# VectorE's order in a pipelined attention: rests, rotations and sums behind the next step's maximum

## The reference

```python
xn = layernorm(x)
s = mamba2_ssd(xn, ...)                     # layer 0, a chunked selective scan
g = silu(moe_top2(xn, ...))                 # 8 experts, 704 wide
x = x + s * g
xn = layernorm(x)
q = rope(xn @ Wq.T); k = rope(xn @ Wk.T); v = xn @ Wv.T     # 32 query heads, 8 key heads, 64 wide
attn = softmax(causal(q @ k.T / 8)); s = (attn @ v) @ Wo.T  # layer 1
g = silu(sign(layernorm(xn) * gamma + beta) @ sign(W - mean(W)).T * alpha + ...)
x = x + s * g
```

## Time and profile before

| | |
|---|---|
| median of 3 runs | 746.0 us (743.95 to 747.15) |
| the profiled execution | 747.68 us, its span 745.9 us |
| mean granted TensorE clock | 0.986 |
| busy, share of the span | TensorE 92%, VectorE 69%, ScalarE 59%, GpSimd 53% |
| attention and tail | from about 326 us to the end |

### The profile page before, as it was taken

The page is one execution under the profiler, slowest core; times in us unless marked ns, Lnnn a source line. Parts: engine busy times, 40 slices in busy tenths (PEclk is TensorE's granted clock), DMA queues, the critical chain, the costliest instruction groups (busy, mean ns, idle before and its releaser), DMA issues.

```text
span 745.9 us, 13421 instructions
## 1 busy us (share of the span) xinstructions
PE 685.3 (92%) x4447; PEld 600.9 (81%) x4448; DVE 514.4 (69%) x1076; ACT 442.0 (59%) x1075; POOL 392.4 (53%) x442
## 2 busy tenths in 40 slices
PE   2999999999999999699879999999999999999886
PEld 2888999989899897687668878788888888887774
DVE  7583656434423426888868878888788888888755
ACT  4446344243242332457767787877877788777762
POOL 1413542423433332137556787777977778776540
PEclk9999999999999999899999999999999999999999
DMA  8175987786878736154442422333323433242001
GB/s 289 48 245 179 293 261 240 249 266 198 266 248 254 224 104 165 28 163 149 106 124 61 111 72 65 99 83 95 82 65 93 93 78 84 56 103 58 15 16 57
DMA packets 108453, 102.25 MB, mean 137 GB/s; under 512 B 51104, under 2 KB 78688, under 8 KB 108256
## 3 DMA queue, kind: packets, MB, share of 16 engines
q1 hardware_dynamic: 106272, 95.62, 44.8%
q0 software_dynamic: 2112, 5.77, 2.4%
HBM read 69.24 MB, written 11.14 MB: 108 GB/s over the span
## 4 chain that ended last, share of the span: by engine, by line
PE 65%; DVE 20%; ACT 5%; issue 5%; POOL 2%; DMA 1%; SPq 1%; DVEq 0%; ACTq 0%
PE bank L1718 14%; PE bank L1752 8%; PE bank L1570 7%; PE bank L1891 5%; DVE p_lo L1083 3%; PE bank L1858 3%; PE bank L1574 3%; DVE o_rest L1092 3%; PE bank L1575 3%; PE bank L1576 3%; DVE nmax L1074 3%; PE bank L1859 3%; DVE q_mix L1040 2%; PE bank L1903 2%; DVE q_mix L1041 2%
## 5 line engine op out<-in xcount | busy, mean ns | idle before, releaser
L1532 POOL TENSOR_TENSOR prob<-prob,rinv 128x128 f32<-128x128 f32 (+3 forms) x256 | 176.4, 721 | 90.5 <-DVE rinv L1079 90.5
L1334 ACT ACTIVATE prob<-bank,nmax 128x512 f32<-128x512 f32 (+3 forms) x256 | 133.3, 526 | 41.4 <-DVE nmax L1074 29.8
L1083 DVE TENSOR_TENSOR p_lo<-bank,p_hi 128x512 fp32r<-128x512 f32 x160 | 109.3, 683 | 59.1 <-ACT p_hi L1341 57.0
L1341 ACT ACTIVATE p_hi<-bank 128x512 fp32r<-128x512 f32 x160 | 95.4, 596 | 48.6 <-PE bank L1570 47.7
L1718 PE MATMUL bank<-xgT,wm 128*128 128x128 f32 x920 | 111.3, 275 | 0.5 <-ACT xgT L1246 0.5
L1718 PEld LDWEIGHTS bank<-xgT,wm 128*128 128x128 f32 x920 | 108.7, 192 | 3.3 <-issue 1.4
L1858 PE MATMUL bank<-kT,qT 128*128 128x512 f32 (+3 forms) x256 | 83.9, 333 | 19.7 <-ACT prob L1334 15.1
L1570 PE MATMUL bank<-cst,prob 128*128 128x128 f32 x640 | 97.3, 275 | 3.2 <-ACT prob L1334 2.5
L1074 DVE TENSOR_REDUCE nmax<-bank 128x1 f32<-128x512 f32 (+2 forms) x192 | 91.0, 501 | 3.6 <-PE bank L1861 3.6
L1891 PE MATMUL bank<-p_lo,v_parts 128*128 128x256 f32 (+3 forms) x288 | 92.1, 343 | 0.1
L1505 POOL DMA_INDIRECT y_rows<-y_row,to_row x21 | 22.7, 1081 | 108.9 <-DVE y_row L943 86.4
(11 more groups left out here) (319 smaller groups left out, 1530.2 us busy)
## 6 DMA issues: line engine op xcount, KB each, us to landing
wm<-in_w_moe SPq DMA_DIRECT2D x23, 1280.0 KB
wm<-in_w_moe SPq DMA_DIRECT2D x23, 640.0 KB, 5.0
qT<-q_hi SPq DMA_DIRECT2D x124, 64.0 KB, 2.0
qT<-q_lo SPq DMA_DIRECT2D x124, 64.0 KB, 2.0
wo_twice<-wo_hi SPq DMA_DIRECT2D x32, 128.0 KB, 2.5
k_exp<-k_rows SPq DMA_DIRECT2D x56, 64.0 KB, 2.0
wtl<-in_w_moe_tail SPq DMA_DIRECT2D x46, 64.0 KB
y_rows<-gate SPq DMA_DIRECT2D x1, 2048.0 KB, 14.0
```

The source lines that it names most:

```text
L1083: TT(p_lo[:, b_, :], bank[2 + b_ % 2][:, :], p_hi[:, b_, :].bitcast(F32), ALU.subtract).then_inc(plo_done, 1)
L1334: ins = actv(prob[:, i % 2, h, POFF[j]:POFF[j] + (j + 1) * P], bk[:, at:at + (j + 1) * P], ACT.Exp, bias=nmax[:, i % 2, h, j:j + 1], accum ...
L1341: actv(p_hi[:, b_, :], bank[2 + b_ % 2][:, :], ACT.Copy).then_inc(phi_done, 1)
L1532: ins = GT(seg, seg, rinv[:, i % 2, k, j:j + 1].to_broadcast([P, (j + 1) * P]), ALU.mult)
```

## The change

The function that makes the lists gets a switch. With it, seven of VectorE's operations whose place is above 3 are put into the next step, at a place between 2.7 and 2.8: behind that step's maximum S (place 2) and reciprocal N (2.6), and ahead of its T (3). Their order among themselves stays. Only VectorE's calls set the switch, and the tail's list isn't changed by it. Each operation keeps its waits, its signals and its instructions; none is added or removed.

```diff
-def schedule(kind):
+AFTER_MAX = ("R", "W", "r", "qa", "ql", "Vl", "Kr")
+
+def schedule(kind, by_max=False):
...
-    picked = [(n - late * STEPS, p, late, op, i, k) for at, late in lists for n, p, op, i, k in at if (n >= STEPS) == late]
+    def placed(n, p, op, i, k):
+        return (n + 1, 2.7 + p / 100, op, i, k) if by_max and kind != "tail" and op in AFTER_MAX and p > 3 else (n, p, op, i, k)
+
+    picked = [(n - late * STEPS, p, late, op, i, k) for at, late in lists for n, p, op, i, k in (placed(*z) for z in at)
+              if (n >= STEPS) == late]
...
-            attend(0, schedule("first"))
+            attend(0, schedule("first", True))
             for gp in range(KVH // 2 - 1):
                 for a in range(2):
-                    attend(gp * 2 + (1 + a), schedule("middle"))
-            attend(KVH - 1, schedule("last"))
-            attend(KVH, schedule("tail"))
+                    attend(gp * 2 + (1 + a), schedule("middle", True))
+            attend(KVH - 1, schedule("last", True))
+            attend(KVH, schedule("tail", True))
```

## The result

The changed kernel takes 752.52 us (median of 4 runs, 752.34 to 753.06), the kernel before, run beside it, 745.74 us (4 runs, 743.95 to 747.15). The ratio is 1.0079 [1.0051, 1.0107]: slower by 0.8%, more than the bound of 0.5%. The forecast was 747.0 and "no change"; "slower" had a chance of 0.20. 752.52 lies at the range's upper edge (752.5).

A forecast was written before the change was run, and what follows sets the result against it. Attention was taken as nearly TensorE's own work, its idle time tracing to maxima late on a full VectorE. Group 0 +3.0, middle +1.0, group 7 and tail -3.0 gave +1.0: 748.7 profiled, 747.0 against the median; range 742 to 752.5.

The forecast's parts named there:

- The signs that the prediction named: Profile after: S3.3 idle near 0.3, new o_rest waits, Q3.1 waiting about 2 us, W0 near 388.5, a half at 23.8.
- The middle groups: Twelve halves of groups 1 to 6, each 0.05 to 0.1 us longer, taken as 0.08: +1.0 us in all.
- The half worked through: Second half of a middle group: S2.4's maximum 1.0 us earlier, S3.0's 0.5 earlier, S3.2's 0.05 later, A2.0 0.6 later.
- the list of thin covers: Middle groups: about 0.2 us spare at R0.0 before A1.0, R1.1 before W0, and T1.4 before T2.1.
- Group 0: Q3.0 0.6 us later, Q3.1 2.3 later behind Kr1.1, W0 2.3 to 2.5 later; +3.0 us, bounds +1.5 and +6.
- the covers I had named at G: Group 0: G of steps 3.0 and 3.1 wait for rotations, covered by 1.79 us of idle time ahead of W0.
- a clock cost on Q3.1: Group 0: a second stall there can bring the 1.2 GHz level again; 0.5 us added.
- Group 7 and the tail: Without rotations maxima first pays: 0.8 us from the first half, 1.5 from the second, plus clock; -3.0, bounds -1 and -4.
- The clock gain: Tail: a shorter wait may keep the clock, up to 1.4 us for 8 matmuls of W; half taken.
- The rests block the value products: Rival, slower: A2.0 of each half waits 0.6 us for R1.0; uncovered, middle groups cost 7.2, time 753.2; chance 0.20.
- The idle time comes back: Rival, faster: the 1.0 us of idle time in each half returns, 12 us in the middle groups, time 734; chance 0.13.
- The order hardly matters: Rival: engines meet at the same semaphores, every term is too small to see, time 746; chance 0.10.

The follow-up runs named there:

- r1_stays: The changed kernel with the second rest of each pair (R1) back in its old place; 748.93 us against 746.01 for the kernel before, ratio 1.0042.
- kr_stays: The changed kernel with the key rotations Kr of group 0 left in their old places; 750.36 us against 746.01 for the kernel before, ratio 1.0049.
- r0_and_first: The changed kernel, but only R0 moves in groups 1 to 7, and all but Kr in group 0; 742.99 us against 747.29 before, ratio 0.9927.
- last_only: The new order in group 7's list alone, all other lists as before the change; 743.86 us against 747.29 for the kernel before, ratio 0.9955.
- rotations: The changed kernel with only r, qa and ql moved; rests, W, Vl and Kr stay; 755.89 us against 747.29 before, ratio 1.0107, 2 runs.
- first_only: The new order in group 0's list alone, all other lists as before the change; 750.02 us against 746.24 for the kernel before, ratio 1.0046.
- rest_and_half_rotation: Group 0 as before; groups 1 to 6 move only R0 and the second rotation r1, group 7 both rests; 740.01 us against 746.24 before, 0.9904.
- rests_stay: The changed kernel with both rests left in their old places, everything else moved; 758.0 us against 746.01 for the kernel before, ratio 1.0161.

## Where the prediction held and where it failed, step by step

The signs that the prediction named came out unevenly. S3.3's idle time (0.27), the waits for `o_rest` and W0 at 388.93 came as forecast. A half is at 24.19 instead of 23.8, just below the 24.2 named as the sign of being wrong, and Q3.1 waits 0.90 us where about 2 was forecast, since Q3.0 ahead of it waits 3.55 (2.29 before). The time lies at the edge of the range, 5.5 us above the forecast; that it does not lie further off supports nothing, since the term that fills it had been put at nothing.

**The middle groups: +1.0 forecast, +5.2 measured. This is the step that failed.** The half worked through stands: S2.4's maximum 0.99 earlier (forecast 1.0), S3.0's 0.52 (0.5), S3.2's 0.03 later (0.05), A2.0's wait 0.63 (0.6), S3.3's idle time 0.27 (0.3), and the end of the half 0.04 later (0.05 to 0.1). What failed is the list of thin covers, "R1.1 some 0.2 us before W0". That margin is right as far as it goes, but W0 is the second that waits for it. R1.1 also frees bank 5, and A2.2 of the same step asks for it 0.57 us ahead of W (529.68 and 530.25 in the kernel before). Before, R1.1 ended at 529.28, 0.40 ahead of A2.2. A waiting product starts 0.14 us behind the end of its rest (533.38 to 533.52), so 0.26 of this was free. Now R1.1 ends 1.23 us behind the start of the step's score (533.38 less 532.15) instead of 0.56, 0.67 later, and A2.2 starts 0.41 later. Nothing behind it in a half takes that up: the first five steps of a half have no idle time, and in the other five VectorE now waits for step 3.0's score (0.48), so that the maxima and exponentials behind it come as late as the score does. So it goes into each half: 0.39 of 0.434 is this wait, and r1_stays shows it: with this one operation back in its place a half is 0.396 shorter. The other 0.04 is the cost that the prediction had worked out (0.08). The description of the kernel names the wait of A2.2 ("A of k = 2 for bank 5"); I looked at the wrong waiter.

**Group 0: +3.0 forecast, +1.1 in the profiled executions, +3.8 when timed alone.** TensorE and its waits in the kernel after, answering to the earlier trace rows:

```profile
357.63 0.66 PE L1580 MATMUL bank<-cst,prob 128*128 128x128 f32 x4 [0.93 <-DVE p_lo L1093]
...
365.81 0.50 PE L1584 MATMUL bank<-xnT_hi,wq_lo 128*128 128x512 f32 x1 [3.55 <-DVE v_all L1051]
371.56 0.50 PE L1584 MATMUL bank<-xnT_hi,wq_lo 128*128 128x512 f32 x1 [0.90 <-DVE v_all L1051]
375.76 0.66 PE L1580 MATMUL bank<-cst,xn 128*128 128x128 f32 x4 [1.13 <-DVE q_mix L1051]
379.11 0.66 PE L1580 MATMUL bank<-cst,xn 128*128 128x128 f32 x4 [1.12 <-DVE q_mix L1051]
...
388.93 0.41 PE L1912 MATMUL bank<-o_rest,wo_twice 128*128 128x512 f32 x1
```

The mechanism is the one forecast in kind: Q3.0 and Q3.1 wait for Kr behind maxima. At the same clock kr_stays takes 1.7 us of the cost away. r0_and_first, without Kr's move, still takes 1.3 us longer than last_only with the old order (64.53 against 63.23), also at the same clock; this part is the queries' rotation and sum, moved ahead of T1.0, and rotations, which moves only these, has Q3.0 waiting 3.04 us. The sizes are not as forecast. I had Q3.0 0.6 later and Q3.1 2.3; they are 2.9 and 3.9. VectorE's rows say why:

```profile
359.46 0.69 DVE L1093 TENSOR_TENSOR p_lo<-bank,p_hi 128x512 fp32r<-128x512 f32 x1 [1.23 <-ACT p_hi L1351]
360.07 0.68 DVE L1080 TENSOR_REDUCE nmax<-bank 128x2 f32<-128x512 f32 x1
360.67 0.74 DVE L1102 SCALAR_TENSOR_TENSOR o_rest<-o_hi,minus,bank 128x512 fp32r<-128x512 f32 x1
361.32 1.98 DVE L1130 TENSOR_TENSOR q_lo<-q_mix,q_hi 128x1024 fp32r<-128x1024 f32 x1
...
364.50 0.65 DVE L1050 TENSOR_TENSOR v_all<-bank,turns 128x512 f32<-128x512 f32 x1
...
368.89 0.75 DVE L1084 TENSOR_REDUCE nmax<-bank 128x1 f32<-128x384 f32 x2 [2.54 <-PE bank L1871]
```

Kr1.0 starts at 364.50 instead of 361.61. Of the 2.9, 0.68 is the maximum with the reciprocal that I counted, 1.45 is T1.0 (359.46 against 358.01, 0.15 of it S0's): the turn ahead of it waited 0.93 us, in the first row of TensorE above, for a lower part that now stands behind a rotation and its sum. And 0.76 is ql2, which took 1.98 us here and 1.22 before. The first W came 2.9 later, near my 2.3 to 2.5, but by another way: no row shows it waiting for the DMAs of `wo_twice` any more. TensorE itself arrives 4.8 later (the score of the next group's step 0.0 at 387.37 against 382.53), the covers I had named at G are used up by 1.13 and 1.12, and the old 1.79 of waiting takes up part of it. That number was right by luck.

The 0.76 us of ql2 are GpSimd's, and the traces show it. Rows of the kernel before, then of the kernel after:

```profile
359.27 1.22 DVE L1120 TENSOR_TENSOR q_lo<-q_mix,q_hi 128x1024 fp32r<-128x1024 f32 x1
359.48 2.13 POOL L1516 TENSOR_TENSOR kT<-k_exp,kT 128x512 fp32r<-128x512 f32 x1 [1.71 <-ACT kT L1319]
```

```profile
360.93 1.29 POOL L1526 TENSOR_TENSOR kT<-k_exp,kT 128x512 fp32r<-128x512 f32 x1 [3.06 <-ACT kT L1329]
```

In all twelve traces the one of the two that starts first keeps its time, and the other ends about 1.1 us behind the first one's end. Where ql2 is first (the kernel before and four others) it takes 1.22 us and GpSimd's kT 1.47 to 2.14; where kT is 0.4 us ahead (the kernel after and six others) kT takes 1.27 to 1.29 and ql2 1.96 to 1.98.

The clock makes up the rest. In the kernel before, behind that wait of 1.79, the granted clock stands at 0.50, the 1.2 GHz level; in the kernel after, W does not wait and it stays at 1.00. Windows of before, then of after:

```profile
388.00:390.00 2.00, 2.00 (x9) 1.88 (x8) 0.80 (x2) 0.00 (x0) 0.81 (x1) 0.50 0.46 112
```

```profile
388.00:390.00 2.00, 2.00 (x15) 1.81 (x15) 1.55 (x5) 2.00 (x7) 0.97 (x2) 1.00 0.72 214
740.00:742.00 2.00, 2.00 (x6) 1.63 (x5) 0.12 (x1) 0.00 (x0) 0.00 (x0) 0.50 0.46 157
```

From the first W to u22 before takes 6.95 us and after 5.29, so 1.66 of the 2.74 come back. I had put a clock cost on Q3.1 (+0.5), which no row shows, and had not looked at what the old wait of W0 already cost. Against an old order that lost no clock there, nothing comes back: S0 to u22 is 63.23 in last_only and 66.50 in first_only, 3.3 apart, and timed, first_only costs 3.8.

**Group 7 and the tail: -3.0 forecast, -1.7 in the profile, -3.4 when timed alone** (ratio of last_only). The order gained less than the 2.3 I had, and most of what is missing is the failed step again: the first half was to hand on 0.8. In last_only step 2.0 does start 0.72 earlier than before, but step 2.1 only 0.32, since A0.2 waits between them for the second rest of the pair before and the step takes 3.79 us instead of 3.39:

```profile
691.84 0.36 PE L1901 MATMUL bank<-p_lo,v_parts 128*128 128x256 f32 x1 [0.16 <-DVE o_rest L1102]
```

The second half adds 1.4 (forecast 1.5). The tail's first turn still waits, 1.67 us where it was 2.46:

```profile
722.58 0.33 PE L1580 MATMUL bank<-cst,prob 128*128 128x128 f32 x1 [1.67 <-ACT prob L1344]
```

The clock gain was right in kind: the window that stood at 0.52 in the earlier trace rows is at full clock in last_only, whose tail takes 26.49 instead of 28.03. In the profiled execution of the kernel after it is not there, because a window at 740 to 742 stands at 0.50 instead; its tail is as long as before (28.04).

**The sum by timed runs.** After less before is 6.8; first_only gives +3.8 and last_only -3.4, so 6.4 are left for the middle groups (5.2 by the timeline). So the sign of the result is made there.

**The rivals.** "The rests block the value products" had the right kind of mechanism and a time of 753.2, close to the measured one, but by another product: the wait of A2.0 it priced is there (0.63) and is covered, as forecast; the one of A2.2 is not. Its chance of 0.20 had been set on the wrong bank. "The idle time comes back" has fallen, and the Trainium skill's rule (Perfetto Trace Analysis, section Identifying Performance Opportunities), to find the gaps of the engine that limits and make what they wait for start sooner, gave 734. Here the named gap did go from 14.1 to 4.4 us, and the time rose by 0.8%: the measurement decides against the rule as it stands, since it does not ask what stands in the queue in the place of the operation pulled ahead. With another choice of operations a part of the idle time does come back: 0.46 us a half in rest_and_half_rotation. "The order hardly matters" has fallen too: the orders tried reach from 740.0 to 758.0.

Not settled: why the timed cost of group 0 (3.8) and the timed rest for the middle (6.4) lie above those of the stages (3.3 and 5.2). The clock and layer 0 wander between executions by more than that.

## What to carry to other kernels

An operation that frees a buffer has as many deadlines as there are operations that wait for it: list all of them, the earliest first, before moving it behind anything, and measure the margin at the first (0.40 us here, less than one maximum of 0.60). On a full engine in a pipeline that repeats, an operation ahead of a waiting one may be what fills the wait; pulling the waiting one ahead turns that into idle time, and only what leaves the stretch altogether is gained. Try the operations of such a change one by one: of seven moved here, the first rest alone gains 0.26 us a half and the second rotation another 0.20, while beside these two the first rotation costs 0.50 (23.297 to 23.793; W and Vl move with it, and they are worth 0.01 by rests_stay and rotations), and the second rest then another 0.40.

## What the runs showed of the hardware that I had not expected

The fall of the granted clock to 0.50 is not tied to the length of the wait ahead of it, and it wanders between executions. Behind Q3.0 in group 0 it came after a wait of 2.90 us in r0_and_first and not after one of 2.90 in kr_stays, which has the same list there, nor after one of 3.04 in rotations. At the tail's first turn it came with a wait of 2.46 us in the kernel before and in first_only, and not with one of 2.46 in rests_stay. And in the kernel after it came within a microsecond of 739.07, where a wait of 1.10 us ends in the tail; the same wait of 1.10 had no fall behind it in last_only.

One fall costs about 1.6 us. From the first W to u22 it takes 6.95 us with it (before) and 5.36 and 5.37 without (last_only, rest_and_half_rotation, both with the old order in group 0); kr_stays and r0_and_first differ by 1.60. In the tail, leaving out its last 3 us, where the clock falls in every execution, those without a fall take 26.5, those with one 27.8 to 28.1 and those with two (r1_stays, rotations) 29.6.

Over all its runs the kernel before scatters from 743.4 to 749.9 us, with mean granted clocks of 0.991 to 0.983, the faster ones at the higher clock. Which falls make that up is not shown, since only one of these executions has a trace. Layer 0 can have a part in it as well: between the traces here S0 differs by 4.1 us.

VectorE and GpSimd held each other up in group 0: of ql2 and kT, which overlap in every trace, the later one took up to 0.8 us longer, as shown above.
